# Cross-attention probabilities turned by VectorE in 32x32 squares and a bounce through memory in place of TensorE, with the projections of a half group spread over four steps

## The reference

```python
x = x + attn(layernorm(x)); x = x + xattn(layernorm(x), ctx, mask); x = x + ffn(layernorm(x))
# xattn: 32 query heads and 8 key/value heads of 128, so four query heads share a key/value head
q, k = rope(q), rope(k)                    # q * cos + rotate_half(q) * sin
scores = where(mask == 0, -1e9, q @ k.T / sqrt(128))
attn = softmax(scores)                     # 8 sequences x 32 heads of 128 x 128
out = (attn @ v) @ Wo
```

## Time and profile before

| | |
|---|---|
| median of three runs | 1030.58 us (1029.69 to 1031.92) |
| the profiled execution: span | 1029.7 us |
| the profiled execution: its own time | the page gives none beside the span; the median is 0.9 us above the span |
| PE busy | 1003.1 us, 97% |
| DVE, ACT, POOL busy | 581.3, 428.1, 381.6 us |
| cross-attention, from the first scores to the end of the last output | 255.1 to 827.3 us |
| one group in the middle of it | 73.0 us |
| the feed-forward behind it | from 828.6 us |

### The profile page before, as it was taken

One profiled execution on the slowest core, in us unless ns is written; L12 is line 12 of the kernel. 1 busy time (PEld: TensorE's weight loads), 2 busy tenths in 40 slices (PEclk: granted clock), 3 DMA queues, 4 the chain that ended last, 5 costly groups with the idle time before them and its releaser, 6 DMA issues. The chain is left out here.

```text
span 1029.7 us, 16071 instructions
## 1 busy us (share of the span) xinstructions
PE 1003.1 (97%) x5260; PEld 822.9 (80%) x5260; DVE 581.3 (56%) x973; ACT 428.1 (42%) x1239; POOL 381.6 (37%) x375
## 2 busy tenths in 40 slices
PE   5999999989999999999999999999999999999998
PEld 3787777876888888888888888888887778888787
DVE  3765555636776666767666666766765852222101
ACT  2777666751533433533533434434334433332100
POOL 7422222253642642643634534626424222222100
PEclk8999999989999999999999999999999999999999
DMA  6000000211110210210210201201100022221001
GB/s 199 12 11 11 11 10 10 62 52 52 50 54 1 73 32 0 71 31 0 74 27 20 72 10 31 61 10 49 43 1 32 1 62 61 61 69 47 11 31 41
DMA packets 45699, 39.98 MB, mean 39 GB/s; under 512 B 3617, under 2 KB 34465, under 8 KB 45665
## 3 DMA queue, kind: packets, MB, share of 16 engines
q1 hardware_dynamic: 45280, 38.48, 12.7%
q0 software_dynamic: 384, 1.05, 0.3%
HBM read 37.43 MB, written 2.10 MB: 38 GB/s over the span
## 5 line engine op out<-in xcount | busy, mean ns | idle before, releaser
L624 PE MATMUL bank<-cross_wo_hl,cross_outT_hl 128*128 128x512 f32 x768 | 191.7, 398 | 1.0 <-POOL cross_wo_hl L618 0.6
L624 PE MATMUL bank<-hsT_hl,cross_wqkv_hl 128*128 128x512 f32 x768 | 188.2, 394 | 0.0
L624 PEld LDWEIGHTS bank<-cross_wo_hl,cross_outT_hl 128*128 128x128 f32 x768 | 143.1, 188 | 35.5 <-POOL cross_wo_hl L618 1.6
L624 PEld LDWEIGHTS bank<-hsT_hl,cross_wqkv_hl 128*128 128x128 f32 x768 | 141.9, 188 | 29.3
L938 ACT ACTIVATE cross_scores<-cross_scores,cross_negmax 128x128 f32<-128x128 f32 x256 | 99.8, 391 | 127.1 <-DVE cross_negmax L876 127.1
L798 POOL TENSOR_TENSOR cross_qT<-rotated,rotated_other_half 128x512 f32<-128x512 f32 x64 | 82.8, 1293 | 162.0 <-DVE rotated_other_half L840 162.0
L624 PE MATMUL bank<-hsT_hl,ff_gate_upT_hl 128*128 128x512 f32 (+1 forms) x528 | 126.3, 395 | 0.5 <-DVE ff_gate_upT_hl L1140 0.5
L624 PEld LDWEIGHTS bank<-hsT_hl,ff_gate_upT_hl 128*128 128x128 f32 (+1 forms) x528 | 96.3, 186 | 21.9 <-DVE ff_gate_upT_hl L1140 0.8
L948 ACT CAST cross_outT_hl<-bank 128x512 fp32r<-128x512 f32 x64 | 37.1, 579 | 143.4 <-PE bank L624 142.5
L838 DVE TENSOR_TENSOR rotated<-bank,cosT 128x512 f32<-128x512 f32 x80 | 55.2, 690 | 71.4 <-PE bank L624 71.2
L624 PE MATMUL bank<-ctxT_hl,cross_wqkv_hl 128*128 128x512 f32 x384 | 94.3, 394 | 1.1 <-PEq L74 1.1
(11 more groups left out here) (121 smaller groups left out, 1565.7 us busy)
## 6 DMA issues: line engine op xcount, KB each, us to landing
staged_rows<-in_wq SPq DMA_DIRECT2D x32, 256.0 KB, 2.8
staged_rows<-in_wo SPq DMA_DIRECT2D x32, 256.0 KB, 2.7
staged_rows<-in_wg SPq DMA_DIRECT2D x10, 256.0 KB, 2.6
staged_rows<-in_wu SPq DMA_DIRECT2D x10, 256.0 KB, 2.8
staged_rows<-in_wd SPq DMA_DIRECT2D x10, 256.0 KB, 3.0
ctx_tok<-in_ctx SPq DMA_DIRECT2D x8, 256.0 KB, 2.6
staged_rows<-in_wk SPq DMA_DIRECT2D x8, 256.0 KB, 3.1
staged_rows<-in_wv SPq DMA_DIRECT2D x8, 256.0 KB, 3.1
```

Source lines behind the costliest of these rows:

```text
L624: i = nc.tensor.matmul(out, stationary[:, a], moving[:, b], start=(first and k == 0), stop=(last and k == 2))
```

## The change

Banks TB and PE's transposes of the probabilities go, and in their place stands a route of seven pieces:

1. DVE transposes each 32x32 square of the scaled probabilities in place (L900 of the changed kernel), SBUF to SBUF, into a new tile of two slots, `turned_blocks_then_probsT`. In step b it does that for b - 1, as its first instruction of the step, ahead of the mask. It waits for `probs2` and for the slot (`probsT_low` of b - 3).
2. SP stores the slot to DRAM (256 KB), waits until that has landed, and reads it back by four transfers of 64 KB that put the squares in their places. `move_blocks` stands in SP's program ahead of the step's weight pieces.
3. ACT makes the high part (L970) from SBUF as the first instruction of step b, for b - 2, ahead of the exponential.
4. POOL makes the low part, also for b - 2, as the first instruction of its step; before, DVE did that.

The transposed probabilities now have their columns in the order (query block, head, query in block), so the two instructions that read the product OB, the high part on ACT and the low part on DVE, read it in runs of 32 numbers to bring the heads back in order. The product itself is the same three matmuls, at the same place, two steps behind the scores.

`blocks_in` now gives the six pieces of a half to four steps: two, one, two, one. v (j = 5) so moves to b = 3 and b = 7. In b = 5 there is one projection only, so the outputs 1 and 2 stand one behind the other. The rows of two norms at the start now use the tile of the scores.

```diff
@@ -744,7 +753,7 @@
 
         def blocks_in(b):
 
-            pairs = {0: (0, 1), 1: (2, 3), 2: (4, 5)}
+            pairs = {0: (0, 1), 1: (2,), 2: (3, 4), 3: (5,)}
             return [(j, 1, 0) for j in pairs.get(b, ())] + [(j, 0, 1) for j in pairs.get(b - 4, ())]
 
         def turns_in(b, last):
@@ -773,8 +782,19 @@
 
         @block.sync
         def _(sp):
-            def body(g, last):
+            def move_blocks(n, slot):
+
+                sp.wait_ge(sem["blocks_turned"], n + 1)
+                sp.dma_start(out_rows[slot], TP[:, slot, :]).then_inc(sem["blocks_stored"], 16)
+                sp.wait_ge(sem["blocks_stored"], 16 * n + 16)
+                for j in range(BLOCKS):
+                    sp.dma_start(TP[j * BLK:(j + 1) * BLK, slot, :].rearrange("c (i f) -> c i f", i=BLOCKS),
+                                 out_rows[slot].rearrange("(i c) (j f) -> j c i f", i=BLOCKS, j=BLOCKS)[j]).then_inc(sem[f"probsT_loaded{slot}"], 16)
+
+            def body(g, first, last):
                 for b in range(SEQS):
+                    if not first or b >= 1:
+                        move_blocks(SEQS * g + b - 1, (b - 1) % 2)
                     for which, ahead, t in turns_in(b, last):
                         if which < PIECES:
                             source = piece_source(io, which, g + 1)
@@ -782,9 +802,11 @@
                             source = io["wo2"][bass.ds((g * QUAD + which - PIECES) * P, P), :]
                         load_piece(sp, m, sem, PIECES + TURNS * g + t, (PIECES + t) % SLOTS, source)
 
-            with sp.Fori(0, GROUPS - 1) as g:
-                body(g, False)
-            body(GROUPS - 1, True)
+            body(0, True, False)
+            with sp.Fori(1, GROUPS - 1) as g:
+                body(g, False, False)
+            body(GROUPS - 1, False, True)
+            move_blocks(SEQS * GROUPS - 1, (SEQS - 1) % 2)
             sp.wait_ge(sem["piece_split"], PIECES + TURNS * (GROUPS - 1) + QUAD)
             load_ff_rows(sp, m, sem, io, 0)
 
@@ -805,6 +827,9 @@
             def body(g, first, last):
                 for b in range(SEQS):
                     n = SEQS * g + b
+                    if not first or b >= 2:
+                        pool.wait_ge(sem["probsT_high"], n - 1)
+                        nc.gpsimd.tensor_tensor(PT[:, 1], TP[:, b % 2, :], PT[:, 0].bitcast(F32), ALU.subtract).then_inc(sem["probsT_low"], 1)
                     for j, half, ahead in blocks_in(b):
                         if j < PIECES - 1 and not (ahead and last):
                             rope_sum(g + ahead, half, j, first=first and not ahead)
@@ -821,6 +846,9 @@
             with pool.Fori(1, GROUPS - 1) as g:
                 body(g, False, False)
             body(GROUPS - 1, False, True)
+            for b in range(2):
+                pool.wait_ge(sem["probsT_high"], SEQS * GROUPS + b - 1)
+                nc.gpsimd.tensor_tensor(PT[:, 1], TP[:, b % 2, :], PT[:, 0].bitcast(F32), ALU.subtract).then_inc(sem["probsT_low"], 1)
             for k in NORM_STATS[SEQS]:
                 norm_rstd(nc, pool, m, sem, k)
 
@@ -865,17 +893,22 @@
                 for b in range(3 if tail else SEQS):
                     n = SEQS * g + b
                     blocks = [x for x in blocks_in(b) if not (x[2] and last)] if not tail else []
+                    if (not first or b >= 1) and (not tail or b < 1):
+                        dve.wait_ge(sem["probs2"], n)
+                        if not first or b >= 3:
+                            dve.wait_ge(sem["probsT_low"], n - 2)
+                        nc.vector.transpose(TP[:, (b - 1) % 2, :].rearrange("p (j h a) -> p h j a", j=BLOCKS, h=QUAD),
+                                            S[:, (b - 1) % 2].rearrange("p h (j c) -> p h j c", j=BLOCKS)).then_inc(sem["blocks_turned"], 1)
                     if not tail:
 
                         dve.wait_ge(sem["scores2"], n + 1)
-                        if not first or b >= 2:
-                            dve.wait_ge(sem["probs_transposed2"], n - 1)
                         nc.vector.scalar_tensor_tensor(out=S[:, b % 2], in0=SC[b % 2][:].rearrange("p (h k) -> p h k", h=QUAD), scalar=SCALE2,
                                                        in1=cap[:, b, :].unsqueeze(1).to_broadcast([P, QUAD, P]), op0=ALU.mult, op1=ALU.min).then_inc(sem["masked2"], 1)
                         dve.wait_ge(sem["masked2"], n + 1)
                         nc.vector.tensor_reduce(negmax[:, b % 2, :], S[:, b % 2], AX.X, ALU.max, negate=True).then_inc(sem["max2"], 1)
                     for j, half, ahead in blocks[:1]:
-                        rope(g + ahead, half, j)
+                        if j < PIECES - 1:
+                            rope(g + ahead, half, j)
                     before, after, late = outputs_in(b, first, last, tail)
                     for y in before:
                         add_output(g, y, first)
@@ -895,11 +928,9 @@
                         nc.vector.reciprocal(rinv[:, b % 2, :], rowsum[:, b % 2, :]).then_inc(sem["rinv2"], 1)
                     if (not first or b >= 2) and (not tail or b < 2):
                         dve.wait_ge(sem["outT_high"], n - 1)
-                        nc.vector.tensor_tensor(oT[:, b % 2, 1], OB[:], oT[:, b % 2, 0].bitcast(F32), ALU.subtract).then_inc(sem["outT_low"], 1)
-                    if (not first or b >= 1) and (not tail or b < 1):
-                        dve.wait_ge(sem["probsT_high"], n)
-                        nc.vector.tensor_tensor(PT[:, 1], TB[(b - 1) % 2][:], PT[:, 0].bitcast(F32), ALU.subtract).then_inc(sem["probsT_low"], 1)
-                    for j, half, ahead in blocks[1:]:
+                        nc.vector.tensor_tensor(heads_of(oT[:, b % 2, 1]), OB[:].rearrange("p (i h a) -> p h i a", i=BLOCKS, h=QUAD),
+                                                heads_of(oT[:, b % 2, 0]).bitcast(F32), ALU.subtract).then_inc(sem["outT_low"], 1)
+                    for j, half, ahead in blocks:
                         if j == PIECES - 1:
                             v_low(g + ahead, half)
                     for y in late:
@@ -932,6 +963,11 @@
             def body(g, first, last, tail=False):
                 for b in range(3 if tail else SEQS):
                     n = SEQS * g + b
+                    if (not first or b >= 2) and (not tail or b < 2):
+                        act.wait_ge(sem[f"probsT_loaded{b % 2}"], 16 * BLOCKS * (HALF * g + (b - 2) // 2 + 1))
+                        if not first or b >= 3:
+                            act.wait_ge(sem["pv2"], n - 2)
+                        nc.scalar.copy(PT[:, 0], TP[:, b % 2, :]).then_inc(sem["probsT_high"], 1)
                     if not tail:
                         act.wait_ge(sem["max2"], n + 1)
                         for h in range(QUAD):
@@ -945,12 +981,7 @@
                         act.wait_ge(sem["pv2"], n - 1)
                         if not first or b >= 4:
                             act.wait_ge(sem["out2"], n - 3)
-                        nc.scalar.copy(oT[:, b % 2, 0], OB[:]).then_inc(sem["outT_high"], 1)
-                    if (not first or b >= 1) and (not tail or b < 1):
-                        act.wait_ge(sem["probs_transposed2"], n)
-                        if not first or b >= 2:
-                            act.wait_ge(sem["pv2"], n - 1)
-                        nc.scalar.copy(PT[:, 0], TB[(b - 1) % 2][:]).then_inc(sem["probsT_high"], 1)
+                        nc.scalar.copy(heads_of(oT[:, b % 2, 0]), OB[:].rearrange("p (i h a) -> p h i a", i=BLOCKS, h=QUAD)).then_inc(sem["outT_high"], 1)
                     if not tail:
                         for j, half, ahead in blocks_in(b):
                             if j == PIECES - 1 and not (ahead and last):
@@ -1051,15 +1082,7 @@
                         if not first or b >= 3:
                             pe.wait_ge(sem["outT_low"], n - 2)
                         products(nc, OB[:], v[:, :, (b - 2) % SEQS, :], PT[:], True, True).then_inc(sem["pv2"], 1)
-                    if (not first or b >= 1) and (not tail or b < 1):
-
-                        pe.wait_ge(sem["probs2"], n)
-                        if not first or b >= 3:
-                            pe.wait_ge(sem["probsT_low"], n - 2)
-                        for h in range(QUAD):
-                            i = nc.tensor.transpose(TB[(b - 1) % 2][:, h * P:(h + 1) * P], S[:, (b - 1) % 2, h, :], ident[:])
-                        i.then_inc(sem["probs_transposed2"], 1)
-                    for j, half, ahead in blocks[1:]:
+                    for j, half, ahead in blocks:
                         if j == PIECES - 1:
                             transpose_v(g + ahead, half)
                     for y in late:
...
```

13 lines of the change are left out of this document (10 added, 3 removed).

## The result

The changed kernel takes 1113.17 us (median of 4 runs, 1112.65 to 1114.26), the kernel before 1030.47 on the same chip: a ratio of 1.0804 (95% interval 1.0789 to 1.082), slower, inside the range of 1050 to 1125 and 13 us above the forecast of 1100. The profiled execution took 1113.52 us with a span of 1111.5; the granted clock is 0.959 in the mean, before 0.992.

What follows compares the result with a forecast made beforehand. The prediction took PE's own work as the bound: a span of 1029.7 us, +53 for groups, start and end, +16 for the clock, gave a span of 1099 and a median of 1100 us; range 1050 to 1125.

Steps and rivals of the forecast that it cites:

- Bound by PE's order: Whole kernel: PE, busy 72.8 of a group's 73.0 us, sets the pace; the order of the engines' work decides.
- PE's own floor of 69.0 us: Each group: 73.0 us less eight steps' transposes of 0.44 and a wait of 0.48, if nothing else waited.
- The transpose of squares, 0.70: DVE, each step: the new transpose takes 0.70 us, with ends of 0.54 and, if two passes, 1.4.
- (a): PV(1) in step 3 of each group: PE waits 5.4 us for POOL's low part of the transposed probabilities.
- (b): Second output of step 5: PE waits 2.5 us for DVE's addition that frees YB.
- (c): v's transposes in step 7: PE waits 1.2 us for ACT's copy of v.
- The start, +10 before the clock: First scores to those of b = 4, first group: 10 us longer, weight pieces being issued only behind the first bounce.
- The end, +6: From the last b = 4 on: PV(3) to PV(7) wait 1 to 3 us each, less transposes saved: +6.
- The clock: Behind each (a) PE's clock falls to the lower level, costing 2 us in each of 8 groups: +16.
- a fallen clock behind (b) as well: Part of the rival of slower new links: +12 us; one or two such parts give 1112 to 1125 us, chance 0.15.
- The sum: Whole span: seven groups +37, start +10, end +6, together +53 on 1029.7 us; with the clock's +16, 1099.
- PE never waits for a bounce except in the first and the last group: Sign in the changed kernel's trace: SP waits often, but the way through memory holds up PE only in those groups.

Runs made afterwards that it cites:

- hybrid: unspread with weight pieces asked for earlier, Wo's parts of step 2 behind the transposed probabilities, TensorE transposing six probabilities at each end: 1021.8 us, ratio 0.9914.
- pool_order: Changed kernel with POOL's three low parts of Wo in step 2 put behind the low part of the transposed probabilities of step 3: 1090.4 us.
- o2_late: Changed kernel with the second output of step 5 moved to step 6, except in the last group: 1090.1 us.
- t_behind: Changed kernel with DVE's transpose of squares behind the mask and maximum of its step, not ahead of them: 1091.8 us.
- no_bounce: Changed kernel without the store to DRAM and the four loads; ACT copies the squares once turned, so the probabilities are not the transposed ones: 1108.9 us.
- fill: Changed kernel with unread matmuls at PE's three longest waits of a group (PV in steps 2 and 3, second output of step 5): 1092.8 us.
- combo2: Changed kernel with the low part on DVE ahead of the transpose, both behind mask and maximum, step 5's second output in step 6, weight pieces asked for earlier: 1063.4 us.
- order_only: hybrid without TensorE's transposes in the first and last group, all 64 transpositions on VectorE: 1040.6 us.
- unspread: Changed kernel with the projections in three steps again, two in each, as before the change: 1086.0 us.

## Why the prediction was right, and where its size was off

- **Bound by PE's order.** Right. PE's own floor of 69.0 us is nearly there: in hybrid 71.56 - 1.65 leaves 69.9.
- **The transpose of squares, 0.70.** 0.709 measured for 128x512 float32. The page "VectorE: DVE Perf Modes" of the Trainium skill, section "The three transpose paths", has 311 ns for one 128x128 bf16; here it is 709 / 4 = 177 ns a square of that size, and the measurement decides.
- **(a) 5.4, (b) 2.5, (c) 1.2.** Measured 5.5, 2.4 and 1.1; pool_order moved (a), o2_late and t_behind moved (b) and (c), along the chains that were walked for them.
- **The start, +10 before the clock.** +10.2 in all, and about 1.8 of it is clock: behind the wait of 6.38 us at PV(0) the windows from 276 to 282 read 0.50, and PV takes 1.62 us, the scores 1.91. So the waits less the transposes saved are 8.4, not 10. The walk put the end of POOL's first three low parts 23 us in; they ended at 23.1. But the bounce, with which it began, is a small part of that: in no_bounce they end at 21.1, and the start is only 1.9 us shorter. What is left comes with POOL's queue: PV(0) waits 4.34 us for it there too.
- **The end, +6.** +11.3. The waits were 0.5 to 3 us, about as said, but the walk left out that the clock falls there too:

```profile
883.96 1.65 PE L626 MATMUL bank<-cross_probsT_hl,cross_v_hl 128*128 128x512 f32 x3 [3.03 <-POOL cross_probsT_hl L832]
885.40 5.11 PE L626 MATMUL bank<-cross_wo_hl,cross_outT_hl 128*128 128x512 f32 x12
```

Against 0.97 and 3.05 at the full clock these two alone are 2.7 us too long; with the other slow rows of the end it is about 5, and 11.3 - 5 is the +6.
- **The clock, "I take 2 us in each of 8 groups ... behind (a) only".** This is the term that was mis-sized, and the words that failed are "behind (a) only". Its 2 us hold: by the lengths of PE's instructions the clock costs 1.7 to 2.7 us behind (a) in seven groups and 1.8 in the first, 16.6 in all. Left out were (b), 1.4 to 1.5 us in six groups, 9.0, and about 4 more in the end. That makes some 30 us where 16 were forecast, about the 13 by which the forecast was too low. fill shows it for the groups; for start and end it is read from rows. The prediction had "a fallen clock behind (b) as well" among its rivals, with 12 us for eight groups. It came, but in six.
- **The sum.** Groups: 69.0 + 5.5 + 2.4 + 1.1 + 3.1 = 81.1 of 81.8; about 0.4 of what is left are first instructions behind a wait, 0.1 longer each. Over 7 groups +61.4 where +37 and 14 of clock were forecast; start +10.2, end +11.3, work outside -1.1: +81.8 on the span. To get from the span to the time the forecast added 0.9 us, the distance of a median to the span of another execution; each execution of either kernel in these runs lies 1.8 to 2.2 us above its own span.
- **"PE never waits for a bounce except in the first and the last group."** Right by no_bounce, in the change's own order. It holds only there: in combo2, where POOL is out of the way, bounce and weight pieces are the next in line.
- **What was not asked.** I priced the spread only through its waits. It has no gain to set against them: alone it costs 15.7 us, in the change 27.

What stays open: whether a middle group can reach 69 us with its transpositions on VectorE (the best, hybrid and order_only, have 71.5 to 71.6), which of their three changes of order gives how much, and why the clock falls behind some waits of one length and not behind others.

## What to carry to other kernels

Work that is taken off the bounding engine brings its time only if what replaces it is not queued behind instructions that wait for something else; walk the new operand through the queue of each engine that it passes, and count the engine's own earlier instructions as part of the wait. Ask of each new wait of TensorE whether the clock falls behind it: it did here behind many waits above 2 us and not behind others, and the work behind it took up to 3.0 us longer (in unspread, behind the 5.62). Where a pipeline fills and drains, a longer chain is paid in full: keep the short chain at the ends, even if the long one wins in the middle.
